# Expert stage of a fused attention and mixture-of-experts layer: the residual is added on the vector engine, with four buffers for the sums, 39 tiles instead of 40, and the tile steps written out

## The reference

```
x = x + attention(layernorm(x), ctx)            # 8 heads of 64, 512 keys
h = layernorm(x) * gamma + beta
shared = silu(h @ sw1) @ sw2.T
probs  = softmax(h @ router_w.T)                # 8 experts
e, p   = argmax(probs), max(probs)
routed = p * (silu(h @ ew1[e]) @ ew2[e].T)      # every token has one expert
x      = x + shared + routed
```

## Time and profile before

| | |
|---|---|
| median of 3 runs | 1043.79 us |
| lowest and highest | 1043.42 and 1045.66 us |
| span of the profiled execution | 1039.1 us |
| PE, DVE, ACT, POOL busy over the span | 83%, 75%, 65%, 32% |
| first scatter of the expert stage starts | 866.85 us |
| last scatter starts | 1029.75 us |

### The profile page before, as it was taken

One profiled execution on the slowest core, in us unless ns is written; L12 is line 12 of the kernel. 1 busy time (PEld: TensorE's weight loads), 2 busy tenths in 40 slices (PEclk: granted clock), 3 DMA queues, 4 the chain that ended last, 5 costly groups with the idle time before them and its releaser, 6 DMA issues.

```text
span 1039.1 us, 26029 instructions
## 1 busy us (share of the span) xinstructions
PE 858.4 (83%) x8816; PEld 715.4 (69%) x8817; DVE 775.2 (75%) x1584; ACT 676.3 (65%) x1541; POOL 335.0 (32%) x335
## 2 busy tenths in 40 slices
PE   3688999989998999899899999999975348666662
PEld 2567878778887878788788978788754226444541
DVE  5387988877887888788788878888772578655563
ACT  4277787776877787777778677887761217554551
POOL 1101122221313221222214121222314345777774
PEclk8799999998999999999999999999996568898886
DMA  5423233241422333242323333241210022222200
GB/s 192 122 62 92 70 95 92 69 109 56 110 75 81 87 98 82 73 112 63 101 71 101 80 91 77 78 113 44 70 32 21 1 69 82 82 85 77 77 31 6
DMA packets 70697, 81.33 MB, mean 78 GB/s; under 512 B 10147, under 2 KB 59821, under 8 KB 70578
## 3 DMA queue, kind: packets, MB, share of 16 engines
q1 hardware_dynamic: 65170, 66.10, 22.7%
q0 software_dynamic: 5408, 13.64, 4.4%
HBM read 35.66 MB, written 13.63 MB: 47 GB/s over the span
## 4 chain that ended last, share of the span: by engine, by line
PE 59%; issue 12%; POOL 10%; DVE 8%; ACT 6%; DMA 2%; SPq 1%; POOLq 0%; ACTq 0%; DVEq 0%
PE FB L336 19%; PE PT L1256 10%; PE S L1246 8%; PE TBK L336 5%; POOL w_hi L568 4%; POOL w_raw L578 3%; PE O L1267 2%; PE O L1269 2%; PE O L1268 2%; POOL out L580 2%; ACT pt_hi L727 2%; ACT probs L733 2%; PE TBK L1330 2%; PE TBK L1331 2%; PE TBK L1323 1%
## 5 line engine op out<-in xcount | busy, mean ns | idle before, releaser
L1091 DVE TENSOR_TENSOR pt_lo<-PT,pt_hi 128x512 f16<-128x512 f32 x256 | 175.4, 685 | 41.2 <-ACT pt_hi L727 36.9
L727 ACT ACTIVATE pt_hi<-PT 128x512 f16<-128x512 f32 x256 | 153.0, 598 | 69.2 <-PE PT L1256 69.0
L1256 PE MATMUL PT<-ident,probs 128*128 128x128 f32 x1024 | 161.6, 281 | 36.2 <-ACT probs L733 22.1
L1078 DVE TENSOR_REDUCE neg_max<-S 128x1 f32<-128x512 f32 x256 | 174.6, 682 | 8.4 <-PE S L1246 8.4
L733 ACT ACTIVATE probs<-S,neg_max 128x512 f32<-128x512 f32 x256 | 177.3, 693 | 3.1 <-DVE neg_max L1078 2.9
L1246 PE MATMUL S<-k_st,q_st 128*128 128x512 f16 x512 | 155.2, 385 | 7.7 <-DMA k_st<-k_stage 7.7
L1256 PEld LDWEIGHTS PT<-ident,probs 128*128 128x128 f32 x1024 | 115.9, 142 | 62.2 <-ACT probs L733 39.1
L336 PE MATMUL FB<-xt_hi,w_hi 128*128 128x256 f32 x384 | 123.9, 323 | 7.3 <-DVE v_st L899 6.8
L1267 PE MATMUL O<-v_st,pt_hi 128*128 128x64 f16 x1024 | 118.4, 195 | 1.1 <-DVE pt_lo L1091 1.1
L1269 PE MATMUL O<-v_st,pt_lo 128*128 128x64 f16 x1024 | 118.0, 194 | 0.0
L1268 PE MATMUL O<-v_st,pt_hi 128*128 128x64 f16 x1024 | 118.0, 194 | 0.0
(11 more groups left out here) (233 smaller groups left out, 2365.1 us busy)
## 6 DMA issues: line engine op xcount, KB each, us to landing
q_st<-q_stage SPq DMA_DIRECT2D x128, 128.0 KB, 2.3
k_st<-k_stage SPq DMA_DIRECT2D x256, 64.0 KB, 2.0
rows<-row SPq DMA_DIRECT2D x16, 512.0 KB, 2.9
w_raw<-in_L_ffn_expert_w SPq DMA_DIRECT2D x15, 512.0 KB, 4.0
c_in<-in_ctx SPq DMA_DIRECT2D x16, 256.0 KB, 2.7
x_in<-in_x SPq DMA_DIRECT2D x16, 256.0 KB, 2.8
xb<-in_x SPq DMA_DIRECT2D x16, 256.0 KB, 2.8
k_st<-in_L_xattn_Wk SPq DMA_DIRECT2D x2, 512.0 KB, 8.1
```

The lines of the kernel that those rows point to most:

```text
L727: a_(pt_hi[(u + 1) % 2][:, :, :], PT[(u + 1) % 2][:, :].rearrange("p (k i) -> p k i", k=KB), ACT.Copy).then_inc(pt_hi_ready, 1)
L1078: v.tensor_reduce(neg_max[:, u % 4:u % 4 + 1], S[u % 2][:, :], AX.X, ALU.max, negate=True)\
L1091: v.tensor_tensor(pt_lo[s][:, :, :], PT[s][:, :].rearrange("p (k i) -> p k i", k=KB), pt_hi[s][:, :, :], ALU.subtract).then_inc(pt_lo_read ...
L1256: last = nc.tensor.transpose(PT[s][:, k * P:(k + 1) * P], probs[s][:, k * P:(k + 1) * P], ident[:, :])
```

## The change

The addition of the residual moves from POOL (L578) to DVE. It becomes `add_residual`, called in step k for tile k - 3, between `through_gate` and `gate_up`. It waits for DVE's own `scale_out` of that tile (`e_y`) and for the scatter of tile a - 4 (`stored`). The sums have four buffers instead of two, and they lie in the tensor `row`. `scale_out` no longer waits for `e_out`. POOL has only scatters and gathers left. There are 39 tiles instead of 40, and all steps are written out instead of partly looped.

```diff
-SLOTS = TILES + E
+SLOTS = TILES + E - 1
 RING = 8
+OUTS = 4
...
-        stored = [sem("stored0"), sem("stored1")]
+        stored = [sem(f"stored{i}") for i in range(OUTS)]
...
             first = lookup({})
-            for k in range(-2, 5):
+            for k in range(-2, SLOTS + 3):
                 step(k, k % RING, k // RING, lambda back, k=k: first(k, k, back))
-            with eng.Fori(0, (SLOTS - RING) // RING) as i:
-                loop = lookup({})
-                for k in range(5, 5 + RING):
-                    step(i * RING + k, k % RING, i + k // RING, lambda back, k=k: loop(i * RING + k, k, back))
-            final = lookup({})
-            for k in range(SLOTS - RING + 5, SLOTS + 3):
-                step(k, k % RING, k // RING, lambda back, k=k: final(k, k, back))
...
-        e_res = [w_raw[:, 2 * D:3 * D], w_raw[:, 3 * D:4 * D]]
+        e_res = [row[:, i // 2, (i % 2) * D:(i % 2 + 1) * D] for i in range(OUTS)]
...
             for a in range(SLOTS):
-                pool.wait_ge(e_y, a + 1)
-                if a >= 2:
-                    pool.wait_ge(stored[a % 2], 16 * (a // 2))
-                g.tensor_tensor(e_res[a % 2], e_yv[a % 2], g_rows[a % RING][:, 0:D], ALU.add).then_inc(e_out, 1)
                 pool.wait_ge(e_out, a + 1)
                 g.indirect_dma_start(out=out, out_offset=bass.IndirectOffsetOnAxis(ap=slot_idx[:, a:a + 1], axis=0),
-                                     in_=e_res[a % 2], in_offset=None,
-                                     bounds_check=B * T - 1, oob_is_err=False).then_inc(stored[a % 2], 16)
+                                     in_=e_res[a % OUTS], in_offset=None,
+                                     bounds_check=B * T - 1, oob_is_err=False).then_inc(stored[a % OUTS], 16)
                 if a + RING < SLOTS:
                     gather(a + RING)
-            for i in range(2):
-                pool.wait_ge(stored[i], 16 * (SLOTS // 2))
+            for i in range(OUTS):
+                pool.wait_ge(stored[i], 16 * len(range(i, SLOTS, OUTS)))
...
             def scale_out(a, s, e):
                 dve.wait_ge(e_down_full, a + 1)
-                if not (is_static(a) and a < 2):
-                    dve.wait_ge(e_out, a - 1)
                 v.scalar_tensor_tensor(e_yv[s], OE[s], slot_prob[:, bass.ds(a, 1)],
...
+            def add_residual(a):
+
+                dve.wait_ge(e_y, a + 1)
+                if a >= OUTS:
+                    dve.wait_ge(stored[a % OUTS], 16 * (a // OUTS))
+                v.tensor_tensor(e_res[a % OUTS], e_yv[a % 2], g_rows[a % RING][:, 0:D], ALU.add).then_inc(e_out, 1)
...
                 if tile_in_range(k - 1):
                     through_gate(k - 1, (r + 1) % 2)
+                if tile_in_range(k - 3):
+                    add_residual(k - 3)
                 if tile_in_range(k - 2):
                     expert(2)
```

## The result

The changed kernel took 984.39 us in the median of 4 runs (979.5 to 984.8), the kernel before beside it 1044.72 (1043.42 to 1049.74). The ratio is 0.9417, 95% interval 0.938 to 0.9454: faster by 5.8%. The profiled execution took 984.8 us with a span of 983.1.

What follows compares the result with a forecast made beforehand. The prediction took POOL, without slack in the second window, as the bound. Last scatter at 866.5 + 38 x 3.1 - 2.5 = 981.8 instead of 1029.75, so 1043.79 - 47.95 = 995.8, forecast 996 us, range 986 to 1012.

Steps and rivals of the forecast that it cites:

- The tile time, 3.1 us: Expert stage, per tile: POOL's mean issues, and DVE's 2.86 with a little lost, give 3.1 us; ends 2.86 and 3.24.
- DVE alone: Rival for the expert stage: DVE sets the pace at 2.86 us a tile, 9.1 us less, 987; chance 0.18.
- long issues: Rival: POOL stays the bound; an issue pair of 3.24 gives 1001 us, one of 3.4 gives 1007; chance 0.12.
- DVE's own pace: DVE's step in the expert stage, with the addition: 2.53 us plus 0.33 to 0.47, so 2.86 to 3.00.
- The thin cover of the load: Expert-number load before `gate_up`: some 0.5 us left for register work; without cover, 0.1 or 0.2 us a tile.
- First scatter 866.5: Start of the expert stage: the first scatter starts at 866.5, tables included, instead of 866.85.
- The tables: Before the expert stage: shorter tables against odd rows, +0.2 us for both; L1033 may lose up to 0.94.
- The end, -2.5: Last tile of the expert stage: runs 3.1 us shorter than in full flow, of which 2.5 is taken off.
- Steps written out, 0: Expert-stage loop: dropping register instructions and repeated loads counted 0, with 0 to 5 x 1.1 us as bounds.
- The sum's base: Whole kernel: saving read from the execution with span 1039.1, taken off median 1043.79; the 4.69 us around left alone.
- Low clock: Rival: PE bounds in stretches at 1.2 GHz; tile 3.43 us and 1008, or 1015 at 5.38 a step; chance 0.20.
- Slower: Rival: every two-operand DVE operation stops POOL's issues, 2.18 us a tile, POOL needs 4.78; 1060 us; chance 0.03.

Runs made afterwards that it cites:

- e12_nogather: The changed kernel with only the first eight gathers made, 31 left out, scatters kept: 981.5 us, ratio 0.9418 (chip 7).
- e13_noscatter: The changed kernel with all gathers but scatters of only the last four tiles: 979.0 us, ratio 0.9395 (chip 7).
- e5_twice: The changed kernel with DVE doing the addition twice, the first time into a spare place: 994.0 us, ratio 0.9547 (chip 12).
- e15_halfcount: The changed kernel with gathers from the ninth on bringing 64 rows instead of 128: 984.4 us (chip 4), 982.2 us (chip 6).
- e1_loop: The changed kernel with the loop of before and 40 tiles, keeping the moved addition and four buffers: 1003.1 us, ratio 0.9658 (chip 4).
- e0_third: The changed kernel unedited, measured again on chip 4: 981.7 us, ratio 0.9452.
- e2_pooladd: The kernel before, written out and with 39 tiles, addition still on POOL, two buffers: 1033.3 us, ratio 0.9932 (chip 8).
- r1_same: The changed kernel with two buffers for the sums instead of four: 999.7 us, ratio 0.9638 (chip 8).
- e8_forty: The changed kernel with 40 tiles instead of 39: 1006.9 us, ratio 0.9662 (chip 7).
- e6_late: The changed kernel with the addition at the end of DVE's step, behind gate_lo: 997.9 us, ratio 0.9566 (chip 12).
- e7_accum: The changed kernel without DVE's addition, the scatter adding to the row in DRAM instead: 998.0 us, ratio 0.9553 (chip 7).
- e14: The changed kernel with gathers from the ninth on bringing 256 floats per row instead of 512: 979.9 us (chip 4), 980.3 us (chip 6).
- e0_again: The changed kernel unedited, measured again on chip 12: 1002.1 us, ratio 0.9629.

## Why the prediction was wrong, by its own steps

*What bounds it, and that POOL's addition was the lever:* right. The 54.2 us of waiting are gone and the stage is 56.46 shorter.

*The tile time, 3.1 us:* this step failed, and it is the larger part of the miss. It took POOL's mean issues from a trace in which POOL was the bound, and added DVE's losses "between engines that are nearly equal". Measured are 2.866, DVE's own step, which also holds where POOL has room (e12_nogather, e13_noscatter) and grows by 0.33 with one addition more (e5_twice). The two issues did not keep their means: the gather fell to 1.04, and the scatter's extra over 1.00 is what is left of `gate_lo` when it starts, less about 0.1: at 887.99, with 0.34 left, it is 0.22. At 959.43 it is 0.59, in a time in which POOL has room: there `split_lo`, also with two operands in SBUF, still ran for 0.10 us, and all of `gate_lo` followed straight behind it. Without such a predecessor an operation that starts that early doesn't count, as the scatter of 1.02 beside `through_gate` shows, and it is a matter of hundredths: e15_halfcount has scatters of 1.02 that start 0.10 before `split_lo` ends. So POOL fits itself into DVE's step. 38 x (3.1 - 2.866) = 8.9 us. It was the rival "DVE alone", priced at 987 and given 0.18; its sign, no gap on DVE, is there. The other sign I named for it, gaps on POOL ahead of scatters, is not, as POOL fills its room with longer issues. POOL without a gap, which I had named as the sign of long issues, came in its place: that sign doesn't tell the two apart.

*DVE's own pace, 2.86 to 3.00, 2.86 taken:* right, and the start-to-start rule (0.33 for the addition from L1119's row) held to 0.01 us; the doubled addition confirms it. *The thin cover of the load:* held in the written out form (0.34 from the addition to `gate_up`), and e1_loop shows that it does not in the loop.

*First scatter 866.5:* 867.39, 0.9 late. It differs between executions: the same kernel has 866.56 in e0_third. *The tables, +0.2 with up to +0.94 for L1023:* it takes 0.54 for 1248 elements against 0.55 for 1280, so the odd rows cost this operation nothing. The sentence by the Trainium skill, "VectorE: DVE Perf Modes", section on mode 2x_1P, would have had +0.7; the trace does not agree. Whether L1023 runs in that mode is not shown.

*The end, -2.5:* 867.39 + 38 x 2.866 - 973.83 = 2.47, but that is in part luck. The last tiles saved 3.1, the value before I shaded it to 2.5, and 0.7 of it was lost by long intervals that the sum hadn't: the first two, of 3.10 and 3.18, and one of 3.06. *Steps written out, 0:* true of the kernel before (0.03 a tile in e2_pooladd), and wrong as a general price: with DVE as the bound it is 12.7 us, which the sum held by starting from a step without register work.

*The sum's base.* This is the second step that failed. The saving was taken off the median 1043.79, although it was read from an execution with a span of 1039.1. In every execution of the changed kernel and its variants the time is 1.7 to 1.9 us above the span (984.8 and 983.1; 1000.58 and 998.9), and in the 29 later ones of the kernel before 1.7 to 2.9. So the 4.69 us "around the span" were mostly the difference between a typical run and a quick one, and the execution that I read lasted about 1041 to 1042. The sum closes with 995.8 - 8.9 + 0.9 - 3.4 = 984.4. Of the 3.4, some 2.9 are this base (with 1.8 around the span), 0.1 is less time behind the last scatter, and 0.4 is the distance of the profiled execution from the median. Either of the two failed steps alone would have left the time inside the range.

*The rivals.* Low clock: refuted, 1.00 in the window; PE got more to do, not less. Long issues: refuted, the tile is 2.87 and not 3.24, and DVE has no gap. Slower, by every two-operand operation stopping POOL: refuted. By the rule of the Trainium skill, "SBUF — State Buffer", section on the two physically separate sides, the loser blocks for the whole instruction; here that holds at the start of an issue and not later in it: four such operations of DVE pass in each tile, and the two issues take 1.22 and 1.04, while DVE's operations keep their 0.41 and 0.68. What none of the rivals had is the late signals of PE. In its first measurement the kernel does not show them, so they are no part of the miss, but they take away 18 of the 60 us on chip 12, and on chips 8 and 7, where the kernel itself was not run, r1_same and e8_forty show 15 and 20 or so.

## What to carry to other kernels

When the bounding engine loses work, the durations of its other operations, read while it was the bound, needn't stay what they were; look for the next engine whose step has no slack (here DVE's own start-to-start sum) and forecast with that. Register work and loads of a loop are free only as long as their engine waits; price them again for the engine that binds afterwards (here 0.03 us a tile became 0.36). And subtract a saving from the execution it was read from, not from a median beside it.

## What the runs showed of the hardware

- On chips 12, 8 and 7 signals of PE come late when gathers and scatters both run and DVE's step is 2.87 or less. In six kernels most signals of `up` are late, in the median by 0.7 to 0.9 us; in e6_late it is 8 of 20, by 1.4, and in e7_accum, in which POOL binds, about half, by 0.3. In the first measurement and on chip 4's e0_third none is (0 of 32 in each), nor on chip 6, where only e14 and e15 ran. Leaving out most of either transfer cures it, breaking PE's train does not. What differs between the chips is open.
- On the same three chips, the events of a scatter's landing are few (900 to 950 us): 2.5 to 4.7 recorded per scatter in the kernels with late signals, 15.5 to 16.1 in the first measurement and on chips 4 and 6. Where the signals are on time there, e12_nogather has 14.8 and e5_twice 10.0. But e2_pooladd has 3.9 and only 1 of 22 signals late by more than 0.1, so the sparse events alone don't make the signals late. Each execution timed here was also recorded, and no run tells whether the recording itself has a part in the late signals.
- More work doesn't bring the late signals: PE is busy 35.61 of 50 us in e0_again, with late ones, and 37.04 in e5_twice, with nearly all on time. A little more work on DVE was faster there.
- The issue of an indirect DMA on POOL waits at its start for a two-operand operation of DVE that still runs, for what is left of it less about 0.1 us, and isn't lengthened by those that start later, except one that follows straight behind the first: 1.22 with 0.34 left in the changed kernel, 1.36 to 1.38 for the gathers of e5_twice, which meet the doubled addition, 0.98 when no such operation runs.
- A scatter that adds to its row in DRAM takes POOL 1.55 us or more to issue, against 0.98 without the addition.
